# Attention scores in four row strips of the array: three rounds of four 32-row matmuls for four 97-row matmuls

## What is computed

```python
q_mag = jax.nn.softplus(q)
k_mag = jax.nn.softplus(k)
q_embed = jnp.stack([q_mag * jnp.cos(qp), q_mag * jnp.sin(qp)], axis=-1).reshape(B_, H, S_, 2 * D)
k_embed = jnp.stack([k_mag * jnp.cos(kp), k_mag * jnp.sin(kp)], axis=-1).reshape(B_, H, S_, 2 * D)
scores = jnp.einsum('bhsd,bhtd->bhst', q_embed, k_embed) / D ** 0.5
attn = jax.nn.softmax(scores, axis=-1)
out = jnp.einsum('bhst,bhtd->bhsd', attn, v)
```

## Time and profile before

| | us |
|---|---|
| median of 3 runs | 1173.82 (1173.16 to 1175.28) |
| profiled execution, span from first to last instruction | 1170.2 |
| attention loop, first to last exponential | 55.0 to 757.1 |
| TensorE / DVE / ScalarE / GpSimd busy | 975.3 / 695.9 / 648.7 / 444.8 |

### The profile page before, as it was taken

One profiled execution on the slowest core, in us unless ns is written; L12 is line 12 of the kernel. 1 busy time (PEld: TensorE's weight loads), 2 busy tenths in 40 slices (PEclk: granted clock), 3 DMA queues, 4 the chain that ended last, 5 costly groups with the idle time before them and its releaser, 6 DMA issues. The chain is left out here.

```text
span 1170.2 us, 15296 instructions
## 1 busy us (share of the span) xinstructions
PE 975.3 (83%) x5541; PEld 570.9 (49%) x5541; DVE 695.9 (59%) x1119; ACT 648.7 (55%) x750; POOL 444.8 (38%) x295
## 2 busy tenths in 40 slices
PE   4597999999998999998999997933378998889870
PEld 2332334444533434533444442422378898889870
DVE  7855275377485267586457642275177656775536
ACT  1276887776776776787776786900123332333224
POOL 3454054053067044048234124034144534444321
PEclk8698999999998999999999998966688988899895
DMA  5597644453646625537626438100434243342228
GB/s 194 180 256 246 155 107 166 108 143 120 154 140 225 154 71 189 115 123 212 164 72 187 107 96 202 46 23 31 160 105 109 48 117 91 105 93 44 23 29 281
DMA packets 72494, 151.85 MB, mean 130 GB/s; under 512 B 9267, under 2 KB 41204, under 8 KB 71632
## 3 DMA queue, kind: packets, MB, share of 16 engines
q1 hardware_dynamic: 52928, 101.59, 32.5%
q0 software_dynamic: 19472, 49.04, 14.7%
HBM read 88.73 MB, written 61.95 MB: 129 GB/s over the span
## 5 line engine op out<-in xcount | busy, mean ns | idle before, releaser
L527 ACT ACTIVATE prob<-spsum 128x1024 f32<-128x1024 f32 x512 | 493.2, 1021 | 177.6 <-PE spsum L665 177.4
L680 PE MATMUL opsum<-prob,val 128*17 128x512 f32 x2048 | 272.2, 603 | 11.3 <-DVE oraw L912 8.8
L665 PE MATMUL spsum<-qst,kst 97*128 97x512 f32 x512 | 157.5, 429 | 15.0 <-issue 9.7
L665 PE MATMUL spsum<-area_q,kst 97*128 97x512 f32 x512 | 156.3, 426 | 2.9 <-issue 2.8
L665 PEld LDWEIGHTS spsum<-qst,kst 97*128 97x128 f32 x512 | 87.8, 192 | 139.3 <-ACT prob L527 98.5
L665 PEld LDWEIGHTS spsum<-area_q,kst 97*128 97x128 f32 x512 | 86.4, 190 | 124.4 <-ACT prob L527 67.6
L448 POOL TENSOR_TENSOR onorm<-oraw,oden 128x512 f32<-128x512 f32 x32 | 45.4, 1418 | 257.1 <-DVE oden L919 257.0
L417 POOL TENSOR_TENSOR square<-raw 128x512 bf16<-128x512 f32 x32 | 59.9, 1871 | 163.5 <-DVE raw L766 163.4
L919 DVE RECIPROCAL oden<-oden 128x256 f32<-128x256 f32 x64 | 112.2, 1753 | 2.2
L1096 POOL DMA_INDIRECT sum_scratch<-eo,add_idx x40 | 62.1, 1553 | 131.3 <-ACT eo L1185 131.3
L1176 ACT ACTIVATE hraw<-hp,b 128x640 f32<-128x640 f32 x64 | 50.9, 796 | 87.0 <-DVE hid L1258 47.4
(11 more groups left out here) (168 smaller groups left out, 1219.0 us busy)
## 6 DMA issues: line engine op xcount, KB each, us to landing
split_scratch<-area_s POOLq DMA_DIRECT2D x56, 512.0 KB, 4.2
kst<-split_scratch SPq DMA_DIRECT2D x45, 512.0 KB, 13.5
area_k<-in_w SPq DMA_DIRECT2D x16, 1024.0 KB, 7.6
qst<-split_scratch SPq DMA_DIRECT2D x24, 512.0 KB, 7.3
area_q<-split_scratch SPq DMA_DIRECT2D x21, 512.0 KB, 7.0
dispatched<-blank POOLq DMA_DIRECT2D x1, 5300.0 KB, 27.3
rows<-dispatched SPq DMA_DIRECT2D x8, 662.5 KB, 4.4
xT<-in_xT SPq DMA_DIRECT2D x4, 1024.0 KB, 16.1
```

The source lines that it names most:

```text
L527: act.activation(prob[u % NPB][:], spsum[u % NSB][:].rearrange("p a n -> p (a n)"), ACT.Exp, scale=HD ** -0.5).then_inc(s_exp, 1)
L665: ins = pe.matmul(spsum[u % NSB][:, e, :], kst[par][:, j, P * kt:P * (kt + 1)], qst[par][:, j, HALF * qh:HALF * (qh + 1)], start=True, sto ...
L680: ins = pe.matmul(opsum[32 * j:32 * j + HD + 1, :], val[b % 2][:, kt, h0 + j, :], prob[(2 * s + j // 2) % NPB][:, HALF * (j % 2):HALF * (j ...
```

## The change

`kst` and `qst` become two views of one tile (`stacks`), with head j in partitions 32j to 32j + 31 and the two parts side by side in the free dimension. A step's scores are three rounds, one for each product; in a round head j's matmul uses rows 32j to 32j + 31, and the rounds add up in `spsum`. Both pairs are announced in the third round. A fill has four transfers of 512 KB. The shift is no row of the stack now but, when needed, a fourth matmul with `row_ones` and `row_max`. Since the shifted scores differ in every step, the branch now encloses all 16 steps of a group, in both arms (`group`). Left out of the diff here: a view in `weight_views`, the place of `TERMS`, the first zero row, and repeated lines of the maxima.

```diff
@@ -29,7 +29,8 @@
 STEPS = 2 * TB
 NG = BATCH * GROUPS
 NSTEP = NG * STEPS
-ROWS = 3 * 2 * HD
+ROWS = 2 * HD
+TERMS = ((0, 0), (0, 1), (1, 0))
 BOUND = 60.0
 ST = CAP // P
 HK = HIDDEN // P
@@ -106,7 +107,7 @@
         ident = sb2("ident", [P, P])
         area_k = sb2("area_k", [P, KC * 2 * SEQ])
-        area_q = sb2("area_q", [P, GH, SEQ], F32R)
+        area_q = sb2("area_q", [P, 2, 2, SEQ], F32R)
         area_s = sb2("area_s", [P, 2 * 2 * 2 * HALF], F32R)
         areas = (area_k, area_q, area_s)
         attention(nc, jobs, number, first, last, x_d, xT_d, wq_d, wk_d, wv_d, wo_d, bias_d, wr_d,
@@ -166,8 +167,10 @@
         over = sb("over", [P, 1])
         flags = sb("flags", [1, NG // 2], I32)
-        qst = [area_q[0:ROWS + 1], sb("qst1", [ROWS + 1, GH, SEQ], F32R)[:]]
-        kst = [sb(f"kst{i}", [ROWS + 1, GH, SEQ], F32R) for i in range(2)]
+        stacks = [area_q[:], sb("stacks1", [P, 2, 2, SEQ], F32R)[:]]
+        qst, kst = [[stack[:, qk] for stack in stacks] for qk in range(2)]
+        row_ones = sb("row_ones", [P, P], F32R)
+        row_max = sb("row_max", [P, SEQ], F32R)
         val = [sb(f"val{i}", [P, TB, HEADS, HD + 1]) for i in range(2)]
         NPB, NSB = 4, 3
         prob = [sb(f"prob{i}", [P, 2 * HALF]) for i in range(NPB)]
@@ -258,8 +261,8 @@
         def filled(eng, grp):
             if grp == 0:
-                eng.wait_ge(s_half, 112)
-            eng.wait_ge(s_fill[grp % 2], 112 * (grp // 2 + 1) - 16 * (grp % 2 == 0))
+                eng.wait_ge(s_half, 64)
+            eng.wait_ge(s_fill[grp % 2], 64 * (grp // 2 + 1))
         def stored(eng, c, i):
@@ -306,10 +309,10 @@
                 for i in (2 * n, 2 * n + 1):
                     stored(sp, 0, i)
                 cols = slice(HALF * n, HALF * (n + 1))
-                for qk, stack, terms in ((0, qst, (0, 0, 1)), (1, kst, (0, 1, 0))):
-                    for r, part in enumerate(terms):
-                        sp.dma_start(stack[0][2 * HD * r:2 * HD * (r + 1), :, cols].bitcast(F32),
-                                     split_d[qk, 0, part, 0:GH, :, cols].rearrange("h r n -> r h n")
+                for qk in range(2):
+                    for part in range(2):
+                        sp.dma_start(stacks[0][:, qk, part, cols].bitcast(F32),
+                                     split_d[qk, 0, part, 0:GH, :, cols].rearrange("h r n -> (h r) n")
                                      ).then_inc(s_fill[0] if n else s_half, 16)
             def fill(grp):
@@ -321,31 +324,25 @@
                 if grp >= 2:
                     sp.wait_ge(s_score, 2 * STEPS * (grp - 1))
-                for qk, stack, terms in ((0, qst, (0, 0, 1)), (1, kst, (0, 1, 0))):
-                    for r, part in enumerate(terms):
-                        sp.dma_start(stack[par][2 * HD * r:2 * HD * (r + 1)].bitcast(F32),
-                                     split_d[qk, b, part, h0:h0 + GH].rearrange("h r n -> r h n")
+                for qk in range(2):
+                    for part in range(2):
+                        sp.dma_start(stacks[par][:, qk, part].bitcast(F32),
+                                     split_d[qk, b, part, h0:h0 + GH].rearrange("h r n -> (h r) n")
                                      ).then_inc(s_fill[par], 16)
-                zero_row(grp, s_fill[par])
                 add_maxima(grp)
-            def zero_row(grp, done):
-                sp.dma_start(qst[grp % 2][ROWS:ROWS + 1].bitcast(F32),
-                             blank[0:GH * SEQ // DIM, 0:DIM]).then_inc(done, 16)
-
             def add_maxima(grp):
-                par = grp % 2
                 sp.wait_ge(s_flag, grp // 2 + 1)
                 flag = sp.value_load(flags[0:1, grp // 2:grp // 2 + 1], min_val=0, max_val=P)
                 with sp.If(flag > 0):
                     sp.wait_ge(g_free, (GEN + 2) * (grp + 1))
-                    filled(sp, grp)
-                    sp.dma_start(qst[par][ROWS:ROWS + 1].bitcast(F32),
-                                 grow[:].bitcast(F32)).then_inc(g_row, 16)
+                    for j in range(GH):
+                        sp.dma_start(row_max[ROWS * j:ROWS * j + 1].bitcast(F32),
+                                     grow[TB * j:TB * (j + 1)].bitcast(F32)).then_inc(g_row, 16)
                 with sp.Else():
-                    sp.sem_inc(g_row, 16)
+                    sp.sem_inc(g_row, 16 * GH)
             def gather_heads(blk):
@@ -393,9 +388,7 @@
         @block.gpsimd
         def _(pool):
-            for i in range(2):
-                pool.memset(kst[i][ROWS:ROWS + 1].bitcast(F32), 1.0).then_inc(s_krow, 1)
-                pool.wait_ge(s_krow, i + 1)
+            pool.memset(row_ones[:].bitcast(F32), 1.0).then_inc(s_krow, 1)
             def clear_slots():
@@ -616,55 +609,78 @@
-            def first_step(grp):
-
-
-                par, s = grp % 2, STEPS * grp
+            def group(grp):
+
+                s0 = STEPS * grp
                 pe.wait_ge(s_flag, grp // 2 + 1)
                 flag = pe.value_load(flags[0:1, grp // 2:grp // 2 + 1], min_val=0, max_val=P)
                 with pe.If(flag > 0):
                     if grp:
-                        values(s - 1)
...
-                                    pe.wait_ge(g_free, base + m)
-                                pe.matmul(misc[:], qst[par][0:ROWS, j, P * t:P * (t + 1)],
-                                          kst[par][0:ROWS, j, HALF * half:HALF * (half + 1)],
-                                          start=True, stop=True).then_inc(g_full, 1)
...
+                        values(s0 - 1)
+                    row_maxima(grp)
+                    for s in range(s0, s0 + STEPS):
+                        scores(s, shifted=True)
+                        for job in jobs_at(s):
+                            run(job)
+                        if s > s0:
+                            values(s - 1)
                 with pe.Else():
                     pe.sem_inc(g_full, GEN + 1)
-                    scores(s)
-                    for job in jobs_at(s):
-                        run(job)
-                    if grp:
-                        values(s - 1)
-
-            def scores(s):
+                    for s in range(s0, s0 + STEPS):
+                        if s == TB // 2:
+                            filled(pe, 0)
+                        scores(s, shifted=False)
+                        for job in jobs_at(s):
+                            run(job)
+                        if s:
+                            values(s - 1)
+
+            def row_maxima(grp):
...
+                            for i, (a, b) in enumerate(TERMS):
+                                ins = pe.matmul(misc[:], qst[par][rows, a, P * t:P * (t + 1)],
+                                                kst[par][rows, b, HALF * half:HALF * (half + 1)],
+                                                start=i == 0, stop=i == 2)
+                            ins.then_inc(g_full, 1)
...
+            def scores(s, shifted):
                 grp, qh, kt = s // STEPS, s // TB % 2, s % TB
                 par = grp % 2
-                for pair in range(2):
-                    u = 2 * s + pair
-                    if u >= NSB:
-                        pe.wait_ge(s_exp, u - NSB + 1)
-                    for e in range(2):
-                        j = 2 * pair + e
-                        ins = pe.matmul(spsum[u % NSB][:, e, :], kst[par][:, j, P * kt:P * (kt + 1)],
-                                        qst[par][:, j, HALF * qh:HALF * (qh + 1)], start=True, stop=True)
-                    ins.then_inc(s_score, 1)
+                cols = slice(HALF * qh, HALF * (qh + 1))
+                for i, (a, b) in enumerate(TERMS):
+                    for j in range(GH):
+                        rows, u = slice(ROWS * j, ROWS * (j + 1)), 2 * s + j // 2
+                        if i == 0 and j % 2 == 0 and u >= NSB:
+                            pe.wait_ge(s_exp, u - NSB + 1)
+                        ins = pe.matmul(spsum[u % NSB][:, j % 2, :], kst[par][rows, a, P * kt:P * (kt + 1)],
+                                        qst[par][rows, b, cols], start=i == 0,
+                                        stop=i == 2 and not shifted)
+                        if i == 2 and not shifted and j % 2 == 1:
+                            ins.then_inc(s_score, 1)
+                if shifted:
+                    for j in range(GH):
+                        u = 2 * s + j // 2
+                        ins = pe.matmul(spsum[u % NSB][:, j % 2, :], row_ones[ROWS * j:ROWS * j + 1],
+                                        row_max[ROWS * j:ROWS * j + 1, cols], start=False, stop=True)
+                        if j % 2 == 1:
+                            ins.then_inc(s_score, 1)
@@ -687,22 +703,18 @@
                     pe.wait_ge(s_free, early)
-                    pe.wait_ge(s_krow, 2)
-                if 0 <= s < NSTEP and s % STEPS == 0:
-
-                    if s:
-                        filled(pe, s // STEPS)
-                    else:
```

(16 more changed lines are left out.)

34 lines of the change are left out of this document (16 added, 18 removed).

## The result

The changed kernel takes **1216.52 us** (median; 1210.18 to 1217.87) beside 1173.49 (1171.83 to 1175.28) for the kernel before on the same chip: ratio 1.037, 95% interval 1.0334 to 1.0405. It is slower by 43 us, where 18 us faster was forecast and 1190 was the upper end of the range. The profiled execution spans 1214.9 us, the clock's mean is 0.897 (before 0.914).

The account below looks back on a forecast made before the run. TensorE was taken to bound the attention loop, ScalarE close behind; scores -23, fills -12 and branch +17 summed to -18 us, from 1173.8 to 1156 us, range 1132 to 1190 (forecast's own range 1142 to 1168).

Parts of the forecast that it names:

- Term 1: Scores matmuls: three rounds of 0.24 us replace four matmuls, saving 11 us in plain and 12 in job steps: -23 us.
- Term 2: Group fills: four 512 KB transfers instead of six land before TensorE needs them, ending waits and some low clock: -12 us.
- Term 3: Group branch: the longer jump must fetch its target, 1.9 us at nine of 16 starts, the others hidden: +17 us.
- X: Cost in us of one far jump at a group's branch, taken as 1.9 between bounds 1.0 and 2.9.
- Rival 2: Group branch: jumps cost more than the change gains, slower above X = 3.1; 1188 us at X = 4; 12%.
- Rivals 1 and 3 to 6: Jump free 1139 us, 13%; slower rounds 1182, 9%; loads in file 1367, 8%; strip-load wait 1265, 4%; strips serial 1653, 4%.
- rival 5: Scores rounds two and three: a strip's weight load waits for that strip's matmul, 0.19 us more each; 1265 us; 4%.

Follow-up runs that it names:

- e1: The changed kernel with the group's untaken arm cut to one step and 64 maxima matmuls, the other 15 steps unshifted behind both arms: 1149.75 us, ratio 0.9825.
- e13: e1 with four more 512 KB transfers in each fill, each onto 128 partitions of a spare tile: 1168.34 us, ratio 0.9972.
- e12: e1 with four more 512 KB transfers in each fill, each onto 32 partitions of a spare tile: 1221.47 us, ratio 1.042.
- e6: e1 with two more 512 KB transfers in each fill, into a spare tile of 128 partitions: 1151.89 us, ratio 0.9862.
- e5: The changed kernel, full function kept: short branch in every step, one-product maxima in the group's branch, values behind a group's first scores when unflagged: 1153.79 us, ratio 0.9863.

## Why the prediction was wrong, point by point

**What bounds the kernel**, TensorE with ScalarE close behind and a two-step loop over values, first result and exponentials: right. Plain steps went from 2.11 to 1.99, and without a round to 1.87, as the working says.

**Term 1 (-23 us): mis-sized, about 0.** Right in the round (0.235 us a slot, loads hidden) and in the plain step's 0.12. Wrong on three counts. Of 93 plain steps 74 were of the 2.11 kind; they gave 5.6 us, 0.12 each in long runs of them and less next to a job, and the other 18 (without the one that waited for DVE) took 2.7 back: 2.9 us, not 11. The 0.24 "in the 50 job steps" did not come: v steps pay 0.20 for the switch from strips to the full array, and turn and router steps hardly moved (on average 2.70 to 2.69 us, 3.10 to 3.08); TensorE waits for DVE's copies in them. And qk cycles, priced at nothing, became longer, 10.58 to 10.78 us; the later first result is the likely reason.

**Term 2 (-12 us): right in the place, wrong in the reason, too small.** The flag loads no longer start with a landing, and 21.7 us went with the short branch, 15.5 at the starts and 6.2 in group 1's wait for DVE. That wait had been taken for something of its own; DVE itself stood 5.4 us for a transfer to the scratch. That it went for the same reason, DMA engines set free, fits the runs (group 1 takes 42.3 us before, 34.0 in e1, 37.6 in e13, 44.6 in e12), though none isolates it. The step that failed is "each 512 KB takes 2.3 us, so four land at 714": it took a transfer's price from its bytes. Onto 128 partitions they land about 1.5 us apart (e1: 691.7, 693.3, 694.8, 696.4), and e6 with six of them was still about as fast as e1 with four.

**Term 3 (+17 us): the mechanism right, its size and cover wrong; this decided.** The bound was 1.0 to 2.9 us, the middle was taken as 1.9, the branch takes 3.3 to 6.9. The sum had the time of the packet itself and of a small load, and no row of a jump. At group 2 the packet starts 1.0 us after the branch and takes 1.15 us (142.33 to 143.48), and TensorE starts 1.6 us behind it; what fills these 1.6 us is not shown. The cover was a mistake of its own: "the 1.88 us of the job cover it" holds for X = 1.9, and with 3.5 the starts with a job ahead stand 1.4 to 1.9 us (group 4):

```profile
236.88 0.97 PE L672 MATMUL spsum<-area_q 32*128 32x512 f32 x12 [1.87 <-issue]
237.78 1.91 PE L696 MATMUL opsum<-prob,val 128*17 128x512 f32 x8
239.62 1.65 PE L672 MATMUL spsum<-area_q 32*128 32x512 f32 x12
```

Two costs were not in the sum. The clock: behind 12 of these pauses it is at its lower level, here with 1.91 and 1.65 instead of 1.05 and 0.97, some 1.5 us for 3.4 us of it. The 27 us more at that level than before make about 12 us (an estimate), though the same effect had been counted in term 2. And the wait for group 1, which was to swallow one jump, was itself about to go. Rival 2 named what happened, with the point of decision at X = 3.1; by its formula X = 3.5 would give 1173.8 - 35 + 41.5 = 1180. The other 36 us are 14 from terms 1 and 2 (21 gained, not 35) and about 12 of clock; branches longer than 3.5 us, further pauses behind the jump and, in the first profile, the pause in group 14 share the rest, which is not divided further.

Two slips stand in the working besides. Nine starts at 1.0 to 2.9 us are 9 to 26 us, not 0 to 26. And the forecast's own low end, 1142 at X = 1.0, lets six groups pay X - 1.9, less than nothing; with nothing for these it is 1173.8 - 35 + 9 = 1148. Neither moves the forecast.

**Rivals 1 and 3 to 6**: refuted by the after trace as above. For rival 5 the rows are plain: the loads of round two start 0.1 us after the matmuls of round one in the same strips (784.85 and 784.75) and run beside them. By the short rule of the Trainium skill, "TensorE: Matmul & The Clock Gate", Part 3, that loads overlap running matmuls only in another row group, the load would wait; the trace disagrees again. The same Part of the Trainium skill also lets a load go ahead into a background weight buffer, which would fit the trace.

## What to carry to other kernels

Count the bytes between a branch and its target as part of the change: below about 20 KB of TensorE's program a taken jump was a third of a microsecond here, above 30 KB 3.3 to 6.9 us whatever the distance, mostly with a slow clock behind it; a short branch in every step cost next to nothing in e5. A transfer here was priced by its shape as well as its bytes, so read GB/s at full DMA engines before counting transfers. And when a matmul is cut into strips, look at what stands next to it: the switch to the full array can cost what the strips save.

## What the runs showed that was not expected

- With the DMA engines about fully busy, 235 GB/s were moved while 512 KB transfers from the scratch went onto 32 partitions, and 322 to 380 while they went onto 128.
- The switch from four strips to a full-array matmul costs 0.20 us at a v job; its first weights are not loaded ahead there.
- The price of a far jump shows no growth from 30 to 74 KB (3.3 to 6.3 us, without order), and 22 KB can be far while 27 KB is near.
- ScalarE pauses with its buffers ready while the DMA engines are full, in step 9 of group 14: 5.96 us in e13, at the end of which, 703.29 to 703.60, a piece of 8 KB of the second instruction queue (q14) came in; ScalarE went on at 704.18. Similar pauses stand in e12 (2.98, 4.54 and 3.13 us) and in one trace of the change (4.72), not in its repetition. That its program came late behind data is a guess from one place; in the pauses of the change's trace there is no such packet. It stays open.
